# Centre rows alternate in a set: spread in two matmuls a quarter, samples written row by row

## The chip, the cores and the metric

The kernel runs on one core of one Trainium2 chip. The metric is device time in microseconds (us) of one execution. TensorE (PE in the rows; PEld is its weight load), VectorE (DVE), ScalarE (ACT), GpSimd (POOL) and SyncE (SP, which issues the DMAs) run side by side and wait for each other by semaphores.

## The reference

The input is 8 images of 32 channels, 128x128, float32. Two blocks follow each other, each with a residual:

```
x = x + L0(gn(x))      # 16 Fourier modes along rows and along columns, and a 1x1 mix
x = x + L1(gn(x))      # modulated deformable 3x3 convolution
```

`gn` with 32 groups of 32 channels is a normalization of each channel of each image. The second block takes nearly all of the time and is what the change touches:

```
om   = conv3x3(x, w_om) + b_om          # 27 channels: 9 dy, 9 dx, 9 masks
ys   = dy + ky + row - 1 ;  xs = dx + kx + col - 1
vals = bilinear(x, ys, xs) * sigmoid(mask)          # for every pixel and tap
out  = einsum('bckhw,ock->bohw', vals, weight) + bias
```

## The kernel before, in words

Images are taken four at a time (`IPG`), two groups (`g_count`), so that 4 x 32 channels fill 128 partitions. After a first stage (statistics, Fourier terms, mix), the second block walks over *sets*. A set is a pair of sample rows (`TILE_R` = 2); there are 65 sets a group (`NSET`), 130 in all. For every set the bilinear sampling is done as matrix products:

- `offsets` (L1025) makes the 27 channels of offsets and masks on TensorE; ScalarE adds the bias into `om_s`; `turn_offsets` (L1029 to L1037) multiplies `om_s` by the 0/1 matrix `perm_s`, which turns pixels into partitions and puts channels in the order wanted. It takes one matmul for each of the two rows. VectorE (L803) subtracts a grid from the result, ScalarE makes hat functions of it (L628, L610), and GpSimd multiplies the hats of y and x (`product`, L485) into `prod`, which VectorE transposes (L761) into `PT`.
- `spread` (L971 to L984) lays the 25 coefficients of a sample out over the positions of a window of 6 x 10 pixels: a product with the 0/1 matrix `sel_s`, which depends on whether the sample's centre row is the first or the second of the tile. It runs three times a set (`ROUNDS`, one for each kx). A set has `ROWS` = 6 *places*, each a pair of output row and ky; `MGROUPS` lists the runs of places that share a centre row: 2, 3 and 1 places. For each run there is a matmul for each half `h` of the columns and each quarter `u` of the partitions, that is 3 x 8. A place has 64 columns (4 images x 16 tiles), so that the runs have 128, 192 and 64. The result goes to `pE` and is copied to `A` by ScalarE (h = 0) and VectorE (h = 1).
- `turn_rows` (L1010 to L1018) transposes windows of the image, four at a time, into `pR`; ScalarE copies them to `XT`.
- `gather` (L987 to L1005) multiplies windows by coefficients: for each tile of 4 pixels, image and half one matmul with 32 output partitions and 72 columns (kx, pixel, place), written next to each other in `pV`. It comes in three parts (`VGROUPS`: 5, 5 and 6 tiles; 80, 80 and 96 recorded matmuls). `evacuate` (L306) tells how ScalarE (L591) and VectorE (L791) copy `pV` to `VS`: they read with a step of 6 elements and write runs of 60 or 72 elements.
- `convolve` (L1039 to L1052) multiplies `VS` by the weights, 36 matmuls of 128 columns; the moving operand is read in runs of 4 elements, 12 apart. VectorE adds bias and residual (L784), and the result is stored.

The kernel is float32 throughout. The trace records each product with data two times, as two weight loads and two matmuls; a transpose is recorded once. The order of TensorE's work in one step is written out by hand in `step` (L1054): spread 0 of set N, convolution of set N-3, gather part 0 of set N-1, turn_rows 0, spread 1, turn_rows 1, offsets of N+3, gather part 1, turn_rows 2, spread 2, turn_offsets of N+3, turn_rows 3, gather part 2. The convolution waits, among others, until VectorE's L803 of the step before has read the bank that it shares (`sub_done`).

The steps are held in two loops, one a group, of 28 iterations with two steps each (`steps`, L270; `UNROLL` = 2); the other 18 sets are written out in straight code before, between and behind the loops.

Of the kernel before, what the change touches and what calls it, by code (L numbers as in the profile page):

```python
# [15 lines left out]
C = 32  # L16
H = W = 128
IPG = 4
P = IPG * C
HW = H * W  # L20
MODES = 16
KS = 3
TAPS = KS * KS
# [3 lines left out]
TILE_R, TILE_C = 2, 4  # L27
WIN_R, WIN_C = TILE_R + 2 * REACH, TILE_C + KS - 1 + 2 * REACH
REG = WIN_R * WIN_C
HALF = P // 2  # L30
# [3 lines left out]
NT = W // TILE_C  # L34
NTP = NT // 2
# [3 lines left out]
OMC = 3 * TAPS  # L39
OMG = IPG * C  # L40
SQ = NSH * NSH
BLK = 32
QUADS = P // BLK
ROWS = KS * TILE_R
PB = ROWS * IPG
# [4 lines left out]
TAPC = KS * TILE_C * ROWS  # L50
# [2 lines left out]
NG = len(VGROUPS)  # L53
PRE = ROWS // 2

MGROUPS = [(0, 2, 0), (2, 5, 1), (5, 6, 0)]

KYS = ((1, 0, 2), (0, 1, 2))
RING = 4
TCH = 4  # L60
TPC = NTP // TCH
# [9 lines left out]
def build(nc, g_count, x, wxr, wxi, wyr, wyi, mixt, mixb, womt, bom, wct, biasc,  # L71
          dft, inv, ident_d, perm, sel, cols, gtab, out):
    ctx = ExitStack()
    with ctx:
        def sb(name, shape, dt=fp32):
            return ctx.enter_context(nc.sbuf_tensor(name, shape, dt))
# [21 lines left out]
        A, VS, XT = areas[0:2], areas[2:4], areas[4:6]  # L98
# [13 lines left out]
        bom_s = sb("bom_s", [OMG, 1])  # L112
        wc = sb("wc", [P, TAPS, 2 * C])
        bias_s = sb("bias_s", [P, 1])
        perm_s = sb("perm_s", [P, TILE_R, OMC * IPG])
        sel_s = sb("sel_s", [P, TILE_R * KS, HALF])
        cols_s = sb("cols_s", [P, 4 + NSH])
        stats = sb("stats", [P, NXC, 6])
# [15 lines left out]
        om_s = sb("om_s", [P, PX])  # L134
# [8 lines left out]
        at = [0]  # L143
# [37 lines left out]
        pV = [pb(f"pV{i}", [P, 512]) for i in range(2)]  # L181
        pMR = pb("pMR", [P, 2 * 512])
        pM, pR = pMR[:, 0:512], pMR[:, 512:1024]
        pO = pMR[:, :].rearrange("p (r n) -> p r n", r=2)[:, :, PX:PX + W]
# [121 lines left out]
        def evacuate(q, gi, h):  # L306

            t0, t1 = VGROUPS[gi]
            x = KS * TILE_C
            dst = VS[q].rearrange("p (m x) -> p m x", m=ROWS)[:, :, (h * NTP + t0) * x:(h * NTP + t1) * x]  # L310
            return dst, pV[h][:, 0:(t1 - t0) * TAPC].rearrange("p (x m) -> p m x", m=ROWS)

        def expanded(q, r, h):

# [17 lines left out]
        def _(sp):  # L332
# [8 lines left out]
            for dst, src in ((dft_s[:, :], dft), (inv_s[:, :], inv),  # L341
                             (wsp[:, 0, :], wxr.rearrange("c o f -> c (o f)")),
                             (wsp[:, 1, :], wxi.rearrange("c o f -> c (o f)")),
                             (wsp[:, 2, :], wyr.rearrange("c o f -> c (o f)")),
                             (wsp[:, 3, :], wyi.rearrange("c o f -> c (o f)")),
                             (cols_s[:, :], cols),
                             (perm_s[:, :, :], perm), (sel_s[:, :, :], sel)):
                sp.dma_start(dst, src).then_inc(const_ld, 16)
            for g in range(1, g_count):
                load_images(g)  # L350
# [2 lines left out]
            for b in range(IPG):  # L353
                r, m = slice(b * C, (b + 1) * C), slice(b * C, b * C + OMC)
# [4 lines left out]
                o = b % 2 * C  # L359
                sp.dma_start(wc[r, :, o:o + C], wct.rearrange("k c o -> c k o")).then_inc(blocks_ld, 16)  # L360
            for ky in range(KS):
                r, k = slice(ky * C, (ky + 1) * C), slice(ky * KS, (ky + 1) * KS)
# [75 lines left out]
            with sp.If(far > 0):  # L438
# [17 lines left out]
                for i in range(images):  # L456
                    m = g_sem[i // IPG]
# [438 lines left out]
        def _(pe):  # L896
            mm = nc.tensor.matmul
# [74 lines left out]
            def spread(n, rn, buf):  # L972

                pe.wait_ge(pt_done, n * ROUNDS + (rn + 1))
                wait(pe, e_act, n * ROUNDS + rn)
                wait(pe, e_dve, n * ROUNDS + rn)
                for first, end, i2 in MGROUPS:
                    for h, u in itertools.product(range(2), range(QUADS)):
                        part = slice(u * BLK, (u + 1) * BLK)
                        src = PT[part, buf, :].rearrange("p (m b t) -> p m b t", m=ROWS, b=IPG)  # L980
                        o = pE[h * HALF:(h + 1) * HALF, u * 512:u * 512 + EPX] \
                            .rearrange("p (m b t) -> p m b t", m=ROWS, b=IPG)
                        last = mm(o[:, first:end], sel_s[part, i2 * KS + rn, :],  # L983
                                  src[:, first:end, :, h * NTP:(h + 1) * NTP], start=True, stop=True)  # L984
                last.then_inc(e_done, 1)

            def gather(n, q, gi):  # L987

                if gi == 0:
                    pe.wait_ge(e_act, n * ROUNDS + ROUNDS)  # L990
                    pe.wait_ge(e_dve, n * ROUNDS + ROUNDS)
                    pe.wait_ge(xt_done, n * TCH + TCH)
                wait(pe, v_act, n * NG + gi)
                wait(pe, v_dve, n * NG + gi)
                pe.nop(nofuse=True)
                t0, t1 = VGROUPS[gi]
                for t in range(t0, t1):
                    o = (t - t0) * TAPC
                    for b, h in itertools.product(range(IPG), range(2)):
                        part = slice(h * HALF, h * HALF + REG)  # L1000
                        at = (b * NTP + t) * TAPC
                        last = mm(pV[h][b * C:(b + 1) * C, o:o + TAPC],  # L1002
                                  XT[q][part, t * P + b * C:t * P + (b + 1) * C],
                                  A[q][part, at:at + TAPC], start=True, stop=True)
                last.then_inc(v_done, 1)  # L1005
# [23 lines left out]
            def turn_offsets(n):  # L1029

                pe.wait_ge(om_act, n + 1)
                for i in range(TILE_R):
                    o = pM[:, 0:OMC * IPG * TILE_R].rearrange("p (f k i b) -> p i f k b", f=3 * KS, k=KS, i=TILE_R)
                    last = mm(o[:, i], om_s[:, i * W:(i + 1) * W],  # L1034
                              perm_s[:, i, :].rearrange("p (f k b) -> p f k b", f=3 * KS, k=KS),
                              start=True, stop=True)
                last.then_inc(omT_done, 1)  # L1037

            def convolve(c, q):  # L1039

                pe.nop(nofuse=True)
                for k, (ky, kx) in enumerate(itertools.product(range(KS), range(KS))):
                    for i, r in itertools.product(range(TILE_R), range(2)):

                        at = TILE_R * KYS[i].index(ky) + i
                        own = at < PRE
                        m = at + PRE if own else at - PRE
                        src = VS[q if own else 1 - q].rearrange("p (m t k j) -> p m t k j", m=ROWS, t=NT, k=KS)
                        part = slice(r * HALF, (r + 1) * HALF)
                        last = mm(pO[i * HALF:(i + 1) * HALF, r, :].rearrange("p (t j) -> p t j", t=NT),  # L1050
                                  wc[part, k, :], src[part, m, :, kx, :], start=(k == 0), stop=(k == TAPS - 1))
                last.then_inc(conv_done, 1)  # L1052

            def step(N, s, on, place):  # L1054
# [68 lines left out]
def constants():  # L1123
# [14 lines left out]
    cols[:, 3] = BN_EPS  # L1138
    cols[:, 4:] = np.arange(NSH) - REACH
    a["cols"] = cols  # L1140
    perm = np.zeros((IPG, BLK, TILE_R, 3, KS, KS, IPG), np.float32)
    for f, kx, i, k, b in itertools.product(range(3), range(KS), range(TILE_R), range(KS), range(IPG)):
        perm[b, f * TAPS + KYS[i][k] * KS + kx, i, f, kx, k, b] = 1
    a["perm"] = perm.reshape(P, TILE_R, OMC * IPG)
    sel = np.zeros((QUADS, BLK, TILE_R, KS, HALF), np.float32)
    for u, sy, sx, i, kx in itertools.product(range(QUADS), range(NSH), range(NSH), range(TILE_R), range(KS)):
        sel[u, sy * NSH + sx, i, kx, (i + sy) * WIN_C + u + kx + sx] = 1
# [36 lines left out]
```

## Time and profile before

| | us |
|---|---|
| median of 2 runs | 2763.61 (2759.2 to 2768.01) |
| profiled execution, device time | 2763.84 |
| its span | 2762.0 |
| PE busy | 2020.7 (73%) |
| PEld busy | 1550.6 (56%) |
| DVE busy | 1338.0 (48%) |
| ACT busy | 1089.8 (39%) |
| POOL busy | 851.8 (31%) |

TensorE is the busiest engine, with 67513 matmuls and as many weight loads of the 153257 instructions of the whole program. Its granted clock was 0.876 of full speed on average. Busy time of matmuls is a union: up to eight that use different parts of the array are in flight together, so the mean time of one (300 ns) says little of how fast they follow each other; the timeline, which merges instructions of a line that follow each other and gives their count, tells that. "Issue" in a chain or behind a row is time in which the engine waited for nothing that the profile shows.

### The profile page before, as it was taken

The page shows a single profiled execution, that of the slowest core. Times are in us where ns is not written, and L with a number is a line of the kernel's source. Part 1 is how long each engine was busy: PE and PEld are TensorE (multiplying, and loading weights), DVE is VectorE, ACT ScalarE, POOL GpSimd, SP SyncE. Part 2 cuts the span into 40 slices and gives each one's busy share as a digit, 9 for nine tenths or more (in the row PEclk, how much of TensorE's full clock was granted, in tenths as well). Part 3 has the DMA queues.
Part 4 walks back from the last instruction along what each step waited for, and adds up shares of the span by engine and source line. Part 5 has one row for each costly group of instructions (what it writes and reads, how often), then busy time and mean ns, then how long its engine had stood idle before and what let it go on. Part 6 is the DMA issues. An engine that isn't in the chain of part 4 may idle for free.

```text
span 2762.0 us, 153257 instructions
## 1 busy us (share of the span) xinstructions
PE 2020.7 (73%) x67513; PEld 1550.6 (56%) x67513; DVE 1338.0 (48%) x2068; ACT 1089.8 (39%) x1858; POOL 851.8 (31%) x893
## 2 busy tenths in 40 slices
PE   8562777767677777777877887777777778777776
PEld 3310555556556655655656665666666556566665
DVE  8694444434444444444444554444444444444453
ACT  0023444334334334334433544444444444444443
POOL 0000433223323333333333443333333333333331
PEclk9697799888888888888888999999989999999998
DMA  7046322212212122122222222222222222222220
GB/s 268 31 192 278 88 66 61 58 52 65 54 52 67 52 54 66 52 53 66 54 64 55 78 69 68 66 56 66 68 54 67 67 68 68 54 67 68 60 64 26
DMA packets 162286, 205.88 MB, mean 75 GB/s; under 512 B 20288, under 2 KB 136672, under 8 KB 157536
## 3 DMA queue, kind: packets, MB, share of 16 engines
q1 hardware_dynamic: 161632, 195.34, 23.9%
q8 instruction: 633, 10.37, 1.7%
q14 instruction: 21, 0.17, 0.0%
HBM read 143.05 MB, written 52.22 MB: 71 GB/s over the span
## 4 chain that ended last, share of the span: by engine, by line
PE 63%; issue 22%; DVE 7%; ACT 3%; DVEq 2%; DMA 1%; ACTq 0%; SPq 0%
PE pV L1002 16%; PE pMR L1050 14%; PE pE L983 12%; PE pMR L1013 9%; PE pMR L1025 7%; PE pMR L1034 3%; DVE big L738 2%; DVE big L761 2%; ACT big L597 2%; DVE big L803 1%; ACT big L610 1%; DMA xh_scratch<-win 1%; DVEq L738 1%; DVE stats L673 1%; PE pV L938 1%
## 5 line engine op out<-in xcount | busy, mean ns | idle before, releaser
L485 POOL TENSOR_TENSOR prod<-big 128x600 f32<-128x600 f32 (+1 forms) x489 | 503.2, 1038 | 1330.2 <-DVE big L761 1316.9
L983 PE MATMUL pE<-big,sel_s 32*64 32x128 f32 (+2 forms) x18720 | 462.2, 302 | 352.0 <-issue 349.7
L983 PEld LDWEIGHTS pE<-big,sel_s 32*64 32x64 f32 x18720 | 365.5, 143 | 453.7 <-issue 427.7
L1002 PE MATMUL pV<-big 60*32 60x72 f32 x33280 | 477.1, 232 | 146.5 <-issue 144.7
L775 DVE COPY big<-pE 128x768 f32<-128x768 f32 x390 | 368.9, 946 | 378.8 <-PE pE L983 370.8
L791 DVE COPY big<-pV 128x360 f32<-128x360 f32 (+1 forms) x390 | 217.4, 557 | 675.1 <-PE pV L1002 675.1
L1002 PEld LDWEIGHTS pV<-big 60*32 60x32 f32 x33280 | 382.8, 106 | 272.0 <-issue 271.0
L604 ACT ACTIVATE big<-pE 128x768 f32<-128x768 f32 x390 | 331.9, 851 | 504.8 <-PE pE L983 503.8
L591 ACT ACTIVATE big<-pV 128x360 f32<-128x360 f32 (+1 forms) x390 | 191.6, 491 | 779.0 <-PE pV L1002 778.9
L1050 PE MATMUL pMR<-big,wc 64*64 64x128 f32 x9216 | 404.2, 339 | 45.9 <-DVE big L803 28.1
L1050 PEld LDWEIGHTS pMR<-big,wc 64*64 64x64 f32 x9216 | 363.8, 176 | 66.6 <-issue 57.4
L1013 PE MATMUL pMR<-ident,big 128*128 128x128 f32 x2080 | 341.6, 285 | 51.2 <-issue 26.6
L761 DVE STREAM_TRANSPOSE big<-prod 128x768 f32<-128x768 f32 x390 | 377.8, 969 | 0.0
L597 ACT ACTIVATE big<-pMR 128x512 f32<-128x512 f32 x520 | 308.0, 592 | 16.3 <-PE pMR L1013 12.8
L1013 PEld LDWEIGHTS pMR<-ident,big 128*128 128x128 f32 x2080 | 223.1, 142 | 100.7 <-ACT big L597 35.4
L515 POOL COPY big<-win 128x960 f32<-128x960 f32 x260 | 248.7, 986 | 0.3 <-DMA win<-xh_scratch 0.3
L1025 PE MATMUL pMR<-big,wom 96*32 96x256 f32 x3120 | 200.3, 389 | 56.1 <-DMA big<-xh_scratch 44.9
L784 DVE SCALAR_TENSOR_TENSOR outs<-pMR,bias_s,x1r 128x256 f32<-128x256 f32 x128 | 62.0, 484 | 273.2 <-PE pMR L1050 273.2
L525 POOL TENSOR_TENSOR big<-big,msk 128x360 f32<-128x360 f32 x130 | 107.0, 823 | 270.4 <-ACT big L628 270.4
L1025 PEld LDWEIGHTS pMR<-big,wom 96*32 96x32 f32 x3120 | 88.2, 110 | 128.8 <-issue 81.2
L803 DVE TENSOR_TENSOR big<-pMR,cols_s 128x720 f32<-128x720 f32 x130 | 116.6, 897 | 50.9 <-ACT msk L637 50.9
L628 ACT ACTIVATE big<-big,cols_s 128x720 f32<-128x720 f32 x130 | 115.3, 887 | 0.0
(70 smaller groups left out, 901.7 us busy)
## 6 DMA issues: line engine op xcount, KB each, us to landing
big<-xh_scratch SPq DMA_DIRECT2D x390, 136.0 KB
win<-xh_scratch SPq DMA_DIRECT2D x130, 408.0 KB, 4.0
xh_scratch<-win SPq DMA_DIRECT2D x32, 544.0 KB, 2.7
big<-in_x SPq DMA_DIRECT2D x16, 1024.0 KB, 15.5
x_scratch<-big SPq DMA_DIRECT2D x16, 1024.0 KB, 3.9
x1r<-x_scratch SPq DMA_DIRECT2D x256, 64.0 KB, 3.3
out<-outs SPq DMA_DIRECT2D x256, 64.0 KB, 2.1
xh_scratch<-zero SPq DMA_DIRECT2D x4, 204.0 KB, 2.7
```

Of the source, the lines that this page charges most:

```text
L485: return nc.gpsimd.tensor_tensor(prod[:, buf, at:at + m, 0:SQ].rearrange("p m (a b) -> p m a b", a=NSH), hy.to_broadcast(shape), hx.to_bro ...
L515: last = nc.gpsimd.tensor_copy(strips[:, 1 - s % 2, :, h, 0:REG].rearrange("p t (r x) -> p t r x", r=WIN_R), tiles_of(1 - s % 2, h))
L597: nc.scalar.activation(XT[q][:, k * 512:(k + 1) * 512], pR[:, :], ACT.Copy).then_inc(xt_done, 1)
L604: nc.scalar.activation(*expanded(q, r, 0), ACT.Copy).then_inc(e_act, 1)
L761: nc.vector.transpose(PT[:, buf, :], prod[:, buf, :, :].rearrange("p m k -> p (m k)")) \
L775: nc.vector.tensor_copy(*expanded(q, r, 1)).then_inc(e_dve, 1)
L791: nc.vector.tensor_copy(*evacuate(1 - q, r, 1)).then_inc(v_dve, 1)
L983: last = mm(o[:, first:end], sel_s[part, i2 * KS + rn, :], src[:, first:end, :, h * NTP:(h + 1) * NTP], start=True, stop=True)
L1002: last = mm(pV[h][b * C:(b + 1) * C, o:o + TAPC], XT[q][part, t * P + b * C:t * P + (b + 1) * C], A[q][part, at:at + TAPC], start=True, st ...
L1013: last = nc.tensor.transpose(pR[:, u * P:(u + 1) * P], strips[:, q, k * TPC + u, :, :].rearrange("p h x -> p (h x)"), ident[:, :])
L1025: last = mm(pM[b * C:(b + 1) * C, 0:PX], wom[:, kx, :], wino[0:KS * C, q, b, :, x0:x0 + W], start=(kx == 0), stop=(kx == KS - 1))
L1050: last = mm(pO[i * HALF:(i + 1) * HALF, r, :].rearrange("p (t j) -> p t j", t=NT), wc[part, k, :], src[part, m, :, kx, :], start=(k == 0), ...
```

## The change

`MGROUPS` and `KYS` go, and `PLACES` lists the six places (output row, ky) so that their centre rows alternate; in `spread` the places 0, 2, 4 share one and 1, 3, 5 the other. So there are two matmuls instead of three for each quarter and half, each of three places, 192 columns. The moving operand and the output step over every other place, in runs of 64 columns in the output.

`turn_offsets` now fills its output in three matmuls (`FILLS`: the row that is turned, and the places that it fills) instead of two, with 108, 72 and 36 columns in place of 108 and 108. `perm_s` has one matrix for both rows.

`gather` writes the samples by place and kx, then column: consecutive output elements of a matmul (the six places) now lie a whole place apart, 60 elements in the parts with 5 tiles and 72 in that with 6. With it `evacuate` reads `pV` in order and writes `VS` in 18 runs of 20 or 24 elements, and `convolve` reads whole rows of 128.

```diff
-MGROUPS = [(0, 2, 0), (2, 5, 1), (5, 6, 0)]
-KYS = ((1, 0, 2), (0, 1, 2))
+PLACES = ((1, 0), (0, 0), (0, 1), (0, 2), (1, 2), (1, 1))
+FILLS = ((0, 1, 4), (1, 4, 6), (1, 0, 1))
...
         def evacuate(q, gi, h):
-            x = KS * TILE_C
-            dst = VS[q].rearrange("p (m x) -> p m x", m=ROWS)[:, :, (h * NTP + t0) * x:(h * NTP + t1) * x]
-            return dst, pV[h][:, 0:(t1 - t0) * TAPC].rearrange("p (x m) -> p m x", m=ROWS)
+            dst = VS[q].rearrange("p (n x) -> p n x", x=W)[:, :, (h * NTP + t0) * TILE_C:(h * NTP + t1) * TILE_C]
+            return dst, pV[h][:, 0:(t1 - t0) * TAPC].rearrange("p (n x) -> p n x", n=ROWS * KS)
...
-                for first, end, i2 in MGROUPS:
+                for i2 in range(TILE_R):
                     for h, u in itertools.product(range(2), range(QUADS)):
-                        last = mm(o[:, first:end], sel_s[part, i2 * KS + rn, :],
-                                  src[:, first:end, :, h * NTP:(h + 1) * NTP], start=True, stop=True)
+                        last = mm(o[:, i2::TILE_R], sel_s[part, i2 * KS + rn, :],
+                                  src[:, i2::TILE_R, :, h * NTP:(h + 1) * NTP], start=True, stop=True)
...
                 for t in range(t0, t1):
-                    o = (t - t0) * TAPC
+                    x = slice((t - t0) * TILE_C, (t - t0 + 1) * TILE_C)
                     for b, h in itertools.product(range(IPG), range(2)):
-                        last = mm(pV[h][b * C:(b + 1) * C, o:o + TAPC],
+                        o = pV[h][b * C:(b + 1) * C, 0:(t1 - t0) * TAPC]                             .rearrange("p (m k x) -> p k x m", m=ROWS, k=KS)
+                        last = mm(o[:, :, x, :],
                                   XT[q][part, t * P + b * C:t * P + (b + 1) * C],
                                   A[q][part, at:at + TAPC], start=True, stop=True)
...
             def turn_offsets(n):
-                for i in range(TILE_R):
-                    o = pM[:, 0:OMC * IPG * TILE_R].rearrange("p (f k i b) -> p i f k b", f=3 * KS, k=KS, i=TILE_R)
-                    last = mm(o[:, i], om_s[:, i * W:(i + 1) * W],
-                              perm_s[:, i, :].rearrange("p (f k b) -> p f k b", f=3 * KS, k=KS),
+                o = pM[:, 0:3 * KS * PB].rearrange("p (f m b) -> p f m b", f=3 * KS, m=ROWS)
+                place_of = perm_s[:, :].rearrange("p (f m b) -> p f m b", f=3 * KS, m=ROWS)
+                for i, m0, m1 in FILLS:
+                    last = mm(o[:, :, m0:m1], om_s[:, i * W:(i + 1) * W], place_of[:, :, m0:m1],
                               start=True, stop=True)
...
-                        at = TILE_R * KYS[i].index(ky) + i
+                        at = PLACES.index((i, ky))
-                        src = VS[q if own else 1 - q].rearrange("p (m t k j) -> p m t k j", m=ROWS, t=NT, k=KS)
+                        src = VS[q if own else 1 - q].rearrange("p (m k x) -> p m k x", m=ROWS, k=KS)
-                        last = mm(pO[i * HALF:(i + 1) * HALF, r, :].rearrange("p (t j) -> p t j", t=NT),
-                                  wc[part, k, :], src[part, m, :, kx, :], start=(k == 0), stop=(k == TAPS - 1))
+                        last = mm(pO[i * HALF:(i + 1) * HALF, r, :], wc[part, k, :], src[part, m, kx, :], start=(k == 0), stop=(k == TAPS - 1))
```

The order of the work in a step, the waits, the loops and the copies' sizes stay as they were.

## Rows read from the trace of the kernel before

**Rows 1.** The page: span, instruction queue, and the chain that ended last.
```profile
span 2762.0 us, 153257 instructions
...
q8 instruction: 633, 10.37, 1.7%
...
PE 63%; issue 22%; DVE 7%; ACT 3%; DVEq 2%; DMA 1%; ACTq 0%; SPq 0%
```

**Rows 2.** Windows: loop 1, loop 2, straight code (start:end, us, busy (x count), clock).
```profile
701.10:1110.60 409.50, 303.13 (x10327) 241.60 (x10324) 176.53 (x240) 162.83 (x280) 130.07 (x135) 0.84 0.22 58
1875.90:2280.40 404.50, 304.98 (x11359) 245.22 (x11352) 190.52 (x264) 175.45 (x308) 143.32 (x150) 0.91 0.24 64
1529.00:1591.40 62.40, 52.23 (x2068) 41.20 (x2069) 34.39 (x49) 31.77 (x57) 26.03 (x27) 1.00 0.27 73
```

**Rows 3.** Timeline of PE, straight code: start, length, what, count [idle before].
```profile
1526.84 0.44 PE L1002 MATMUL pV<-big 60*32 60x72 f32 x19 [1.07 <-issue]
1527.20 0.91 PE L983 MATMUL pE<-big,sel_s 32*64 32x128 f32 x48
1528.95 2.20 PE L1050 MATMUL pMR<-big,wc 64*64 64x128 f32 x72 [0.83 <-issue]
1531.08 1.08 PE L1002 MATMUL pV<-big 60*32 60x72 f32 x80
1532.08 0.66 PE L1013 MATMUL pMR<-ident,big 128*128 128x128 f32 x4
1532.67 0.79 PE L983 MATMUL pE<-big,sel_s 32*64 32x128 f32 x28
1534.46 0.66 PE L983 MATMUL pE<-big,sel_s 32*64 32x192 f32 x20 [1.00 <-issue]
```

**Rows 4.** Timeline of PE in loop 1, around the loop's jump.
```profile
1102.19 0.33 PE L1002 MATMUL pV<-big 60*32 60x72 f32 x8 [2.19 <-issue]
1106.50 1.34 PE L983 MATMUL pE<-big,sel_s 32*64 32x128 f32 x25 [3.98 <-issue]
1109.50 1.12 PE L983 MATMUL pE<-big,sel_s 32*64 32x192 f32 x23 [1.66 <-issue]
...
1126.05 0.89 PE L983 MATMUL pE<-big,sel_s 32*64 32x128 f32 x42 [1.63 <-issue]
```

**Rows 5.** Timeline of PE in loop 2, an iteration's second set and the jump.
```profile
2260.70 2.32 PE L1050 MATMUL pMR<-big,wc 64*64 64x128 f32 x72 [0.97 <-DVE big L803]
...
2265.44 0.49 PE L1013 MATMUL pMR<-ident,big 128*128 128x128 f32 x3 [1.15 <-issue]
...
2271.16 0.69 PE L1034 MATMUL pMR<-perm_s,om_s 128*128 128x108 f32 x4
2271.69 0.60 PE L1013 MATMUL pMR<-ident,big 128*128 128x128 f32 x4
...
2273.37 0.89 PE L1002 MATMUL pV<-big 60*32 60x72 f32 x65 [0.68 <-issue]
2278.91 1.59 PE L983 MATMUL pE<-big,sel_s 32*64 32x128 f32 x48 [4.65 <-issue]
```

**Rows 6.** Groups of instructions by form: count, busy us, mean ns, idle before.
```profile
L1002 PE MATMUL pV<-big 60*32 60x72 f32 x33280 | 477.1, 232 | 146.5 <-issue 144.7 <-DVE big L791 1.4
...
L983 PE MATMUL pE<-big,sel_s 32*64 32x192 f32 x6240 | 278.3, 357 | 51.9 <-issue 51.0
...
L983 PE MATMUL pE<-big,sel_s 32*64 32x128 f32 x6240 | 218.1, 315 | 287.4 <-issue 286.1 <-DVE big L775 0.8
...
L983 PE MATMUL pE<-big,sel_s 32*64 32x64 f32 x6240 | 178.1, 234 | 12.7 <-issue 12.6
...
L791 DVE COPY big<-pV 128x360 f32<-128x360 f32 x260 | 138.4, 532 | 388.8 <-PE pV L1002 388.8
...
L803 DVE TENSOR_TENSOR big<-pMR,cols_s 128x720 f32<-128x720 f32 x130 | 116.6, 897 | 50.9 <-ACT msk L637 50.9
...
L791 DVE COPY big<-pV 128x432 f32<-128x432 f32 x130 | 79.0, 607 | 286.3 <-PE pV L1002 286.3
```

More of the change, by code:

```diff
@@ L114, in build @@
         bias_s = sb("bias_s", [P, 1])
-        perm_s = sb("perm_s", [P, TILE_R, OMC * IPG])
+        perm_s = sb("perm_s", [P, 3 * KS * PB])
         sel_s = sb("sel_s", [P, TILE_R * KS, HALF])
@@ L346, in _ @@
                              (cols_s[:, :], cols),
-                             (perm_s[:, :, :], perm), (sel_s[:, :, :], sel)):
+                             (perm_s[:, :], perm), (sel_s[:, :, :], sel)):
                 sp.dma_start(dst, src).then_inc(const_ld, 16)
@@ L1140, in constants @@
     a["cols"] = cols
[L1141 to L1144, printed above, removed]
+    perm = np.zeros((IPG, BLK, 3, KS, ROWS, IPG), np.float32)
+    for f, kx, m, b in itertools.product(range(3), range(KS), range(ROWS), range(IPG)):
+        perm[b, f * TAPS + PLACES[m][1] * KS + kx, f, kx, m, b] = 1
+    a["perm"] = perm.reshape(P, 3 * KS * PB)
     sel = np.zeros((QUADS, BLK, TILE_R, KS, HALF), np.float32)
```

## The prediction

> **What bounds the kernel now.** I read the page first: its chain of work that ended last is 63% PE and 22% "issue" [rows 1]. So TensorE carries the end, and a fifth of the span it stands still without waiting for a semaphore that the profile shows. Where these stops lie, the timeline of PE tells. Some stand at a change of work; the longest of the others come in the middle of a run of equal matmuls that depend on nothing new: 1.07 us inside gather part 2, then 1.00 us inside spread 1 [rows 3]. Between these two stand 19+48+72+80+4+28 = 251 matmuls with as many weight loads, 502 recorded instructions, and by the code some ten waits and register instructions. The instruction queue moved 10.37 MB in 633 packets [rows 1], 16.4 KB each, and 10.37 MB over 153257 instructions is 68 bytes for each. So a packet carries about 250 instructions (my estimate: 64 bytes, 256 instructions, as the profile does not record all), and the stops are two packets apart. I read them as TensorE running dry: its code is streamed anew each time round, and a dense stretch of small matmuls eats a packet faster than the next one comes. The windows give the pace: straight code takes 62.4 us for 4 sets at full clock, 15.6 us a set, 15.1 ns for each of the 4137 matmuls and loads. Loop 2 takes 404.5 us for 22 sets, 36.8 us an iteration of two, at clock 0.91; loop 1 409.5 us for 20 sets, 41.0 us an iteration, at clock 0.84 [rows 2]. Both loops run the same work. What differs is the stops: at the jump back PE waits 3.98 us in loop 1 and 4.65 us in loop 2, but loop 1 stops besides for 2.19 us eight matmuls ahead of the jump, for 1.66 us 25 matmuls behind it, and for 1.63 us in the next spread 0 [rows 4]; loop 2 shows 1.15 and 0.68 us in its second set [rows 5]. With 2.19 and 3.98 us of rest nearly on end, TensorE falls to the lower of its two clock levels (a mean of 0.84 is two thirds of the time at 2.4 GHz and one third at 1.2).
>
> **What the change takes away, in instructions.** Spread has 24 matmuls a round and gets 16, each recorded as two loads and two matmuls: 3 rounds x 8 x 4 = 96 fewer. turn_offsets gets one matmul more, +4. That is 92 of about 1034 recorded instructions a set [rows 2], or 8.9%; an iteration goes from about 2118 (waits included) to 1934.
>
> **Spread on TensorE itself.** A round lasts from 1527.20 to 1528.11, 0.91 us [rows 3]. Its columns stay the same: 16 x (128+192+64) = 6144 = 32 x 192 (16 recorded matmuls for each of the three old groups, 32 new). If instructions set its length, it loses 16 x 19 ns = 0.3 us; if columns do, nothing. Gather passes 80 matmuls from 1531.08 to 1532.08, 12.5 ns each [rows 3], with as many loads, so 48 could pass in 0.6 us; and 128 more columns raise the mean of one from 234 to 357 ns [rows 6]. It is columns, and I take 0. A gain in spread 0 would in part be lost anyway: convolution behind it waits for VectorE's L803, 0.97 us [rows 5], and that comes from the end of gather part 2 by a copy of 607 ns and 897 ns of L803 [rows 6], whatever spread does.
>
> **turn_offsets.** Four matmuls of 108 columns take 2271.16 to 2271.69, 0.53 us [rows 5], 133 ns each; the transposes with 128 columns take (1532.67 - 1532.08)/4 = 148 ns [rows 3]. Two more cost from 0 (hidden in a wait for code) to 2 x 133 ns = 0.27 us a set, 35 us in all. Nearest is 0.15 us, and it lies in a stretch that runs dry before or behind it, so I charge 0.1 us a set in straight code and put it into the loops' sums below.
>
> **Evacuation and convolution.** The copy of 360 elements takes 532 ns, that of 432 takes 607 [rows 6]: 1.04 ns an element, with PSUM read at a step of 6. L803, which reads each PSUM value in place, takes 897 ns for 720: (897-607)/288 = 1.01 ns. A read in order saves 0 to 0.03 x 360 = 11 ns; I take 0. Convolution's 72 matmuls took 2.20 us [rows 3], 31 ns each; the whole-row read saves from 0 to the gap to what its columns need. At the rate of spread, 0.91 us / 6144 = 0.148 ns a column with eight tiles in flight, four tiles need 0.296 x 128 = 38 ns. It is faster already, so 0.
>
> **Gather's strided write.** The trace before has no matmul whose neighbouring outputs lie apart one by one. Lower bound: nothing. The nearest row is turn_offsets, which writes runs of four elements with gaps, and at 133 ns for 108 columns it is not slower than the transposes that write in order. Upper bound: a write that halves or quarters the rate of columns. At 0.148 ns a column the 72 columns need 10.7 ns of the 12.5 that a matmul now takes. Twice that is 21.3 ns, +8.8 x 256 = +2.3 us a set; four times is 42.6 ns, +7.7 us a set. I take no cost, since neither the read with a step (L791) nor the write with gaps (turn_offsets) shows one. The Trainium skill ("PSUM — Partial Sum Buffer", section Specifications (TRN2)) speaks against that: it gives PSUM lines of 8 bytes and says that any non-contiguous pattern slows matmuls significantly. The rows of turn_offsets show no such cost for runs of 16 bytes; of single elements no row here tells. By the rows the sum is the 2595 below, by the page the first rival's 2725 to 3430.
>
> **Where the stops go.** The saving is in waiting for code, and in the straight code it is 92 x 15.1 ns = 1.4 us a set less the 0.1 above: 1.3 us, within the roughly 2 us of stops in a set [rows 3]. 18 sets give -23 us.
>
> In the loops the place of the packets' boundaries decides. Loop 1 runs dry 25 matmuls into an iteration, about 53 instructions with the waits, and then 53 + 8 x 256 = 2101, which is the stop eight matmuls ahead of the end at 2118 [rows 4]: the reading holds. Before loop 1 lie 5 sets with spread and 8 turn_offsets, so its start moves forward in the code by 5 x 96 - 8 x 4 = 448 = 256 + 192 instructions, and its first boundary comes 192 later in it: at 245, and the last to 1781, 153 ahead of the jump. Both costly stops (2.19 + 1.66 us) fall away, the jump's stays. Of the others (1.63 us) about half goes. The clock gains as well: a third of an iteration is now at half rate, and with 3.9 us less rest about 2.5 us of it should go, worth 1.2 us of work. Sum: -3.85 - 0.8 - 1.2 + 0.2 (turn_offsets) = -5.7 us an iteration, x 28 = -160 us.
>
> Loop 2 runs dry after one transpose of its second set's turn_rows 0 [rows 5], instruction 1475, so its first boundary is at about 190. Its start moves forward by 448 + 184 + 9 x 92 = 1460 = 5 x 256 + 180 instructions, so its first boundary goes to 190 + 180 - 256 = 114, and the last one to 1906, 28 ahead of the jump at 1934: where loop 1 has its 2.19 us now. So loop 2 gains some 2.0 us of other stops (1.15, 0.68 and their like in its first set) and pays 2.2 us and some clock for the new place: +0.5 us, x 28 = +14 us.
>
> Together -23 - 160 + 14 = -169 us. Against the profiled execution's span of 2762.0 that is 2593; 1.8 us lie around it (2763.84, and the median of the runs is 2763.61), so 2595.
>
> The Trainium skill ("Runtime: NRT & Kernel Launch", section Instruction fetch mechanics) says that code comes in blocks of 256 instructions, that crossing one is mostly hidden and that a taken branch breaks the prefetch. The trace agrees on the blocks and on the jump (3.98 and 4.65 us), not on "hidden".
>
> **Rivals.** *First, the write is slow.* It needs the single strided elements to cost where groups of four do not. At twice the columns' time, +2.3 us a set less about 1.3 us of stops that it fills, +130 us: 2725. It decides for "slower" (over 2819) when a set pays 1.7 us beyond what the stops cover: 3.0 us / 256 = 11.7 ns more, 24 ns a matmul, 2.3 times the columns' 10.7. At four times, +6.4 x 130: 3430. If the array's columns are cheaper than spread suggests, twice is almost covered by the stops: 2625.
>
> *Second, the stops are not code.* If "issue" were a cost that each place has in itself, 92 fewer instructions would only move it to L803 (0.97 us) and to ScalarE's copies; then about 0.3 us a set is left: 2725. Against it: the same work has other stops in each loop, two packets apart.
>
> *Third, boundaries fall elsewhere than counted.* The shift rests on counted instructions. Worst, both loops get loop 1's present places, with two packets' worth less to wait for: -2.0 and +2.2 us an iteration, 2745. Best, both get good ones: loop 2 gains 3 us, 2500.
>
> **Numbers.** Forecast as worked out (2520 to 2660) 0.48; its better end 0.07; the write at up to twice 0.16, half of it still over 2% faster; the write at 2.3 times or more 0.14; stops not code or boundaries badly placed 0.15, a third of it over 2% faster. Faster by over 2% (2708): 0.48 + 0.07 + 0.08 + 0.05 = 0.68; slower 0.14; within 2% 0.18. A measurement of this kernel tells less than 2% from no change with difficulty. The range, 2500 to 2800, leaves out the slow write and the best tail.
>
> **What would show it.** L983 with 12480 matmuls, all of 192 columns, and a round still near 0.9 us; L1034 with 6 a set; L1002 still 12.5 ns a matmul in the timeline (near 21 if the write is slow, with a mean well over 232 ns); fewer packets on the instruction queue, about 633 - 130 x 92 / 256 = 586; loop 1 near 35 us an iteration with no stop just ahead of the jump, loop 2 near 37 with one. I am wrong if L1002's runs grow, or if the stops keep their sum.

## The result, and the profile after

| | us |
|---|---|
| before, median | 2763.61 |
| changed, median of 2 runs | 2620.68 (2619.18 to 2622.18) |
| ratio | 0.948, 95% interval 0.941 to 0.955 |
| span of the profiled execution | 2617.3 |

The change makes the kernel 5.2% faster; 2595 was forecast. The page of the changed kernel has 11960 instructions fewer, 62 packets less on the instruction queue (its columns: packets, MB, share), and a chain with 19% of "issue" where before had 22% [rows 1]:

```profile
span 2617.3 us, 141297 instructions
...
q8 instruction: 571, 9.36, 1.5%
...
PE 65%; issue 19%; DVE 8%; ACT 4%; DVEq 2%; DMA 1%; ACTq 0%; SPq 0%
```

The same three kinds of stretch as in [rows 2], each laid along whole iterations: 20 sets of loop 1, 22 of loop 2, 4 of the straight code (columns: start:end, us, busy and count of PE, PEld, DVE, ACT and POOL, granted clock, DMA share, GB/s).

```profile
582.00:946.90 364.90, 287.62 (x9404) 221.43 (x9404) 174.40 (x240) 160.76 (x281) 130.12 (x135) 0.88 0.25 64
1805.90:2210.00 404.10, 311.15 (x10346) 231.73 (x10345) 190.49 (x265) 176.64 (x309) 143.31 (x150) 0.92 0.24 64
1360.20:1421.00 60.80, 52.29 (x1891) 39.20 (x1887) 34.60 (x49) 32.20 (x57) 26.79 (x28) 1.00 0.28 77
```

An iteration of loop 1 takes 36.5 us in place of 41.0; one of loop 2 36.7 as before (36.8); a set of the straight code 15.2 in place of 15.6. Over all 26 iterations between the first and the last jump back, loop 1 takes 36.25 us in place of 41.05 and loop 2 36.8 in both. So of the 145 us of span 126 (28 x 4.5, by the windows) to 134 (28 x 4.8, by all iterations) come out of loop 1 alone and nothing out of loop 2. What is left, 12 to 19 us, is put down to the 18 sets written out, 0.6 to 1.0 us each; the four of the window show 0.4.

TensorE's own work has hardly changed, as the groups by form show against [rows 6]: a gather matmul, which now writes elements 60 or 72 apart, takes 232 ns as it did, and the copy that now reads in order takes 532 ns as it did.

```profile
L1002 PE MATMUL pV<-big 60*32 60x72 f32 x33280 | 470.7, 232 | 89.4 <-issue 87.1 <-DVE big L790 1.6
L982 PE MATMUL pE<-big,sel_s 32*64 32x192 f32 x12480 | 429.6, 365 | 319.3 <-issue 318.4 <-DVE big L774 0.8
...
L790 DVE COPY big<-pV 128x360 f32<-128x360 f32 x260 | 138.4, 532 | 383.9 <-PE pV L1002 383.9
```

Timeline of PE around the jump of loop 1 (start, length, line, count, idle before):

```profile
924.04 0.87 PE L982 MATMUL pE<-big,sel_s 32*64 32x192 f32 x20
926.44 0.57 PE L982 MATMUL pE<-big,sel_s 32*64 32x192 f32 x12 [1.53 <-issue]
...
937.16 0.91 PE L982 MATMUL pE<-big,sel_s 32*64 32x192 f32 x32
937.99 0.86 PE L1035 MATMUL pMR<-perm_s,om_s 128*128 128x108 f32 x6
938.68 0.63 PE L1013 MATMUL pMR<-ident,big 128*128 128x128 f32 x4
939.25 1.31 PE L1002 MATMUL pV<-big 60*32 60x72 f32 x96
945.12 1.59 PE L982 MATMUL pE<-big,sel_s 32*64 32x192 f32 x32 [4.56 <-issue]
```

Against [rows 4] the stop of 2.19 us eight matmuls ahead of the jump and that of 1.66 us behind it are gone: gather's 96 and spread's 32 run through. The stop at the jump is longer, 4.56 in place of 3.98 us, and the one in the next spread 0 is still there (1.53, was 1.63). And of loop 2:

```profile
2018.71 1.11 PE L1002 MATMUL pV<-big 60*32 60x72 f32 x85
2022.38 0.34 PE L1002 MATMUL pV<-big 60*32 60x72 f32 x11 [2.56 <-issue]
2026.62 1.59 PE L982 MATMUL pE<-big,sel_s 32*64 32x192 f32 x32 [3.90 <-issue]
...
2042.52 0.69 PE L1002 MATMUL pV<-big 60*32 60x72 f32 x41 [0.52 <-issue]
```

Here is the new stop, 11 matmuls ahead of the jump: 11 x 2 recorded instructions and the waits behind them, where the count of the prediction had put it (28 instructions). It stands there, 11 matmuls ahead, at all 27 jumps of this loop, and lasts from 0.3 to 2.8 us, 1.84 us in the mean. With it the stop at the jump is shorter, 3.90 in place of 4.65 us [rows 5]. The last row is the same part of gather in the next iteration's first set: the count has a boundary there too, 114 + 3 x 256 = 882 instructions behind the jump.

### The profile page after: what moved, and what is told of

Read it like the earlier page. It is cut to its first block, busy times and chain, and to the rows that moved or that the text cites. A ratio compares the mean times of both kernels' runs of the same rounds, so it can differ in the third digit from the quotient of the medians.

```text
span 2617.3 us, 141297 instructions
## 1 busy us (share of the span) xinstructions
PE 1998.2 (76%) x61533; PEld 1456.0 (56%) x61533; DVE 1332.1 (51%) x2068; ACT 1088.3 (42%) x1858; POOL 851.8 (33%) x893
## 4 chain that ended last, share of the span: by engine, by line
PE 65%; issue 19%; DVE 8%; ACT 4%; DVEq 2%; DMA 1%; ACTq 0%; SPq 0%
PE pV L1002 17%; PE pMR L1050 15%; PE pE L982 11%; PE pMR L1013 9%; PE pMR L1025 7%; PE pMR L1035 4%; DVE big L737 2%; ACT big L596 2%; DVE big L760 2%; DVE big L802 1%; ACT big L609 1%; DMA xh_scratch<-win 1%; DVEq L737 1%; DVE stats L672 1%; PE pV L937 1%
## 5 line engine op out<-in xcount | busy, mean ns | idle before, releaser
L982 PE MATMUL pE<-big,sel_s 32*64 32x192 f32 x12480 | 429.6, 365 | 319.3 <-issue 318.4
L1002 PE MATMUL pV<-big 60*32 60x72 f32 x33280 | 470.7, 232 | 89.4 <-issue 87.1
L982 PEld LDWEIGHTS pE<-big,sel_s 32*64 32x64 f32 x12480 | 252.5, 142 | 405.6 <-issue 391.0
L1050 PEld LDWEIGHTS pMR<-big,wc 64*64 64x64 f32 x9216 | 356.2, 174 | 107.5 <-issue 107.1
L1013 PEld LDWEIGHTS pMR<-ident,big 128*128 128x128 f32 x2080 | 229.8, 146 | 105.8 <-ACT big L596 63.4
L1035 PEld LDWEIGHTS pMR<-perm_s,om_s 128*128 128x128 f32 x780 | 98.9, 194 | 40.1 <-issue 35.5
## 6 DMA issues: line engine op xcount, KB each, us to landing
big<-in_x SPq DMA_DIRECT2D x16, 1024.0 KB, 15.5
```

The costliest lines, as they stand in the source:

```text
L982: last = mm(o[:, i2::TILE_R], sel_s[part, i2 * KS + rn, :], src[:, i2::TILE_R, :, h * NTP:(h + 1) * NTP], start=True, stop=True)
L1002: last = mm(o[:, :, x, :], XT[q][part, t * P + b * C:t * P + (b + 1) * C], A[q][part, at:at + TAPC], start=True, stop=True)
L1013: last = nc.tensor.transpose(pR[:, u * P:(u + 1) * P], strips[:, q, k * TPC + u, :, :].rearrange("p h x -> p (h x)"), ident[:, :])
L1050: last = mm(pO[i * HALF:(i + 1) * HALF, r, :], wc[part, k, :], src[part, m, kx, :], start=(k == 0), stop=(k == TAPS - 1))
```

## The experiments

Each stands beside runs of the kernel before on its own chip; the chips differ (before took 2766.4, 2739.3 and 2797.6 us on the three), so ratios are compared, or kernels of the same call.

**The layouts apart from the spread.** First the changed kernel with the old gather, copies and convolution:

```diff
-            return dst, pV[h][:, 0:(t1 - t0) * TAPC].rearrange("p (n x) -> p n x", n=ROWS * KS)
...
+            return dst, pV[h][:, 0:(t1 - t0) * TAPC].rearrange("p (x m) -> p m x", m=ROWS)
...
-                        last = mm(o[:, :, x, :],
+                        last = mm(pV[h][b * C:(b + 1) * C, o:o + TAPC],
...
```

> The changed kernel with gather, evacuation and convolution as they were before: the samples are written next to each other, the copies read PSUM with a step of 6, the convolution reads runs of 4. The instruction count and every packet boundary are those of the changed kernel. If fewer instructions make the gain: 2620 us as changed, within 15. If the rows layout brings part of it (a faster copy or convolution), this one is slower than 2620 by that part; if the strided write costs something that the gain hid, it is faster than 2620.

Measured: 2597.51 us, ratio 0.939 (0.937 to 0.942), 8 us below the range of 2620 within 15. Then the other half, the kernel before with the new layouts alone:

> The kernel before with only the rows layout (strided gather write, copies in order, convolution of whole rows); spread keeps its three groups and turn_offsets its two matmuls. Instruction count as before. If fewer instructions make the gain: as before, 2763 us within 15. If the layout makes it: near 2620. If the strided write costs and was hidden: above 2780.

Measured: 2767.0 us beside 2766.44, ratio 1.0006 (0.9991 to 1.0022), over ten runs. So all of the gain is with the spread (and the third matmul of turn_offsets that belongs to it), and the layouts bring nothing. Its gather, written with a stride, and its copy, against [rows 6]:

```profile
L1002 PE MATMUL pV<-big 60*32 60x72 f32 x33280 | 472.0, 231 | 144.9 <-issue 143.4 <-DVE big L790 1.3
...
L790 DVE COPY big<-pV 128x360 f32<-128x360 f32 x260 | 138.4, 532 | 373.6 <-PE pV L1002 373.6
```

231 ns for a matmul and 532 for a copy: nothing in either. The first run left a question, as it was faster than the changed kernel had been. So that was run again:

> The changed kernel itself, timed beside the others. 2620 us if the 23 us by which the kernel with alternating spread alone was faster (2597.5) belong to the rows layout; 2600 to 2610 if they are a matter of the day and the few runs.

Measured: 2582.41 us, below both values, but on a chip on which before took 2739.29, so that only the ratio speaks: 0.942 (0.939 to 0.945). The intervals of 0.939 and 0.942 overlap; by these two runs a cost of the strided write of up to some 0.7% can't be told from none. The run before them, on one chip, leaves 0.2%, and both layouts were timed beside each other again below, without loops.

**The code moved, nothing changed.** The kernel before with 60 transposes more while TensorE waits for the images anyway:

```diff
             pe.wait_ge(ident_ld, 16)
+            for _ in range(120 // 2):
+                nc.tensor.transpose(pM[:, 0:P], ident[:, :], ident[:, :])
```

> The kernel before, with 60 transposes of the identity (120 instructions, about 8 us of TensorE's time while it waits for the images) ahead of everything, which moves the code of both loops by 119 instructions against the packets and changes nothing in them. Loop 1's first boundary goes from 53 to 190, its last from 19 to 136 ahead of the jump, which is where loop 2 has them now; loop 2's goes from 190 to 71. If the place of the boundaries sets the stops: loop 1 41.0 -> about 37 us an iteration, loop 2 36.8 -> about 38.5, together about 2690 us (2660 to 2730). If only the number of instructions counts, or the columns: as before, 2763 within 10.

Measured: 2737.15 us, ratio 0.990 (0.987 to 0.993): faster by 1.0%, but above the range of 2660 to 2730. Windows over 20 sets of each loop:

```profile
582.78:960.93 378.15, 280.68 (x10325) 223.73 (x10320) 173.20 (x240) 158.53 (x280) 130.02 (x135) 0.89 0.24 62
1787.62:2179.57 391.95, 302.11 (x10324) 244.35 (x10320) 176.30 (x240) 162.36 (x280) 129.99 (x135) 0.85 0.23 60
```

The loops have changed places: loop 1 takes 37.8 us an iteration (was 41.0), loop 2 39.2 (was 36.8), with not one instruction in them changed. 120 instructions at the start of the program are worth 3.2 us an iteration one way and 2.4 us the other. That the stops come where packets end is shown by this. The sum was expected at 2690, since loop 1 was put at about 37 and loop 2 at its new boundary (71) at 38.5. The timeline of loop 2 shows why it came out at 39.2:

```profile
1792.04 1.54 PE L985 MATMUL pE<-big,sel_s 32*64 32x128 f32 x37 [4.36 <-issue]
1795.07 0.50 PE L985 MATMUL pE<-big,sel_s 32*64 32x64 f32 x11 [1.49 <-issue]
```

After 4.36 us at the jump TensorE gets through 37 matmuls and stands again for 1.49 us: a first boundary soon behind the jump costs a second stop. It does so behind each of the 27 jumps of this loop (1.1 to 1.8 us) and of loop 1 before (1.4 to 1.9 us): the packets' own times in the traces show that the next packet begins only 0.3 to 1.0 us after TensorE goes on.

These times show the cause directly. Every packet of the instruction queue has 16384 bytes. In the kernel before, between 500 and 2200 us, all 165 stops of over 0.3 us in the middle of a run of equal matmuls end 2.2 to 3.0 us after the last packet began; a packet takes about 1.1 us (median), and TensorE goes on 1.2 to 1.7 us after it has landed. In the two kernels without loops that follow below, the packets begin at least 3.3 us apart between 500 and 2200 us, 3.9 and 4.0 us in the median, so that one is under way at a time.

**The third matmul put back.** The changed kernel, all layouts and the order of places kept, but three places cut into 2 and 1:

```diff
-                for i2 in range(TILE_R):
+                for i2, first, end in ((0, 0, 4), (1, 1, 6), (0, 4, 5)):
...
-                        last = mm(o[:, i2::TILE_R], ...
+                        last = mm(o[:, first:end:TILE_R], ...
```

> The changed kernel with spread's first group of three places cut in two (2 and 1 places), so that there are again 24 matmuls of 128, 192 and 64 columns: the instruction count of before plus 4 a set, columns, layouts and the order of the places as changed. If instructions make the gain: 2780 us (2750 to 2810), loop 1 near 41 us an iteration with a stop at its start, loop 2 near 37.3. If the alternating places or the row layout make it: 2620.

Measured: 2810.32 us, ratio 1.017 (1.013 to 1.021), at the upper end of the range. All of the gain is gone and 44 us more, which are loop 2's. Loop 1 is back at 40.6 us an iteration, loop 2 at 38.9 with its first boundary at 114 (37.3 was expected):

```profile
611.39:1017.71 406.32, 302.37 (x10370) 245.55 (x10360) 174.33 (x240) 161.81 (x280) 130.04 (x135) 0.84 0.22 58
1874.80:2263.82 389.02, 296.42 (x10362) 242.50 (x10360) 174.30 (x240) 160.95 (x280) 130.03 (x135) 0.86 0.23 61
```

The columns are those of the changed kernel, so the gain is one of instructions and not of how the places lie. But the boundaries in the loops have moved with the count, and this run doesn't tell the two apart; the kernels without loops do.

**Loop 2 moved in the changed kernel.** Matmuls of one spread are issued again in a straight set between the loops (they write the same values once more):

```diff
-                    spread(N, 0, q)
+                    spread(N, 0, q, 44 if isinstance(N, int) and N == NSET else 0)
```

> The changed kernel with 44 matmuls of 64 columns of one spread issued again in straight code between the loops (176 instructions, about 1 us once), which moves loop 2's code and nothing else: its first packet boundary goes from 114 to 194, its last from 28 ahead of the jump to 204. If the place of the boundaries sets the stops, the stop of about 1.8 us in gather part 2 ahead of the jump goes and loop 2 falls from 36.8 to about 34.5 us an iteration: 2560 us (2545 to 2590). If the place doesn't matter: 2621.

Measured: 2615.49 us, ratio 0.955 (0.954 to 0.957), where the changed kernel had 0.942 on the same chip: 33 us or 1.3% slower, not faster. This was a miss. The windows (loop 1, which didn't move, and loop 2, ten iterations each) give 36.1 and 36.9 us an iteration:

```profile
575.47:936.04 360.57, 283.21 (x9400) 216.60 (x9400) 174.31 (x241) 160.49 (x281) 130.07 (x135) 0.90 0.24 65
1719.70:2088.63 368.93, 287.70 (x9400) 221.54 (x9400) 173.34 (x241) 161.00 (x281) 130.10 (x135) 0.88 0.24 63
```

On that chip the changed kernel took 35.9 and 35.8:

```profile
465.23:824.64 359.41, 284.70 (x9400) 218.43 (x9400) 174.15 (x241) 160.39 (x281) 130.08 (x135) 0.89 0.24 65
1601.76:1959.70 357.94, 281.77 (x9400) 210.56 (x9400) 173.17 (x241) 160.26 (x281) 130.06 (x135) 0.92 0.24 66
```

So the 33 us are loop 2's. Its timeline (gather is L1010 in this kernel) shows what it has in place of the stop ahead of the jump:

```profile
1742.09 0.25 PE L1010 MATMUL pV<-big 60*32 60x72 f32 x1 [2.49 <-issue]
...
1761.98 1.58 PE L982 MATMUL pE<-big,sel_s 32*64 32x192 f32 x32 [4.91 <-issue]
```

The stop ahead of the jump has gone, but that at the jump is 4.91 us and not 3.90, and inside the iteration a boundary now falls one matmul ahead of gather's end, behind the densest run of instructions, and costs 2.49 us (1.93 in the mean). A boundary close ahead of the jump is thus no loss by itself: it makes the jump's own stop shorter. All 27 jumps of each loop show it, with the packets that begin while TensorE stands there:

| loop | last boundary ahead of the jump, instructions by the count | stop at the jump, median (range), us | packets that begin |
|---|---|---|---|
| before, loop 1 | 19 | 3.60 (3.4 to 4.0) | 1 |
| changed, loop 2 | 28 | 3.72 (3.4 to 4.0) | 1 |
| third matmul put back, loop 1 | 57 | 3.64 (3.3 to 3.9) | 1 |
| before, loop 2 | 136 | 4.77 (4.6 to 5.1) | 2 |
| before and moved, loop 1 | 136 | 4.94 (4.6 to 5.5) | 2 |
| changed, loop 1 | 153 | 4.95 (4.4 to 5.8) | 2 |
| changed and moved, loop 2 | 204 | 4.67 (4.1 to 5.3) | 2 |
| third matmul put back, loop 2 | 220 | 4.51 (4.0 to 5.1) | 2 |
| before and moved, loop 2 | 255 | 4.32 (3.6 to 5.0) | 2 (at two jumps 1) |

A packet that begins alone takes about 1.1 us; the second of two, which begins 0.5 to 1.1 us behind the first (medians of the loops), takes 1.6 to 2.0, and TensorE goes on about 1.7 us after it has landed in either case. So the stop is longer because the packet that ends it begins behind another or is slower beside it. That the first of them is the code behind the loop's end, fetched for nothing, is my reading; the traces don't say which code a packet holds.

**Fewer jumps.** Four sets to an iteration on TensorE:

```diff
-            steps(pe, step, UNROLL)
+            steps(pe, step, RING)
```

> The changed kernel with four sets to an iteration in TensorE's loops in place of two; the other engines' loops as they are. 28 jumps fewer. An iteration of two sets takes 36.2 and 36.8 us in the loops and 30.4 in straight code, so a jump costs about 6.1 us with the slow clock behind it. If jump and fetch bind: 2620 - 28 x 6.1 = 2450 us (2410 to 2500). If the stop at the jump is a wait for another engine's work, which would come late elsewhere too: above 2550.

Measured: 2454.26 us, ratio 0.897 (0.894 to 0.900). That it lies next to the 2450 expected is luck: this chip is faster than the one that the sum started from. Beside the changed kernel's 2582.41 us here, 28 jumps fewer give 128 us and not 170, that is 4.6 us a jump and not 6.1. And none at all:

```diff
-            steps(pe, step, UNROLL)
+            for N in range(-3, SETS + 2):
+                live = [0 <= N + k < SETS for k in (0, -1, -3, 3, 2, 1, -2)]
+                live[2] = live[2] and (N - 3) % NSET < NPAIR
+                live[6] = live[6] and (N - 2) % NSET < NPAIR
+                step(N, N % RING, live, lambda n: divmod(n, NSET))
```

> The changed kernel with TensorE's 133 steps all written out, no loop; the other engines' loops as they are. If the jumps and the clock that falls behind them are what the loops add: 112 sets at 15.2 us in place of 18.3, 2620 - 347 = 2275 us (2240 to 2350), clock near 1.0 throughout. If code that is never run twice is fetched more slowly, or another engine is next: above 2400.

Measured: 2281.28 us, ratio 0.833 (0.831 to 0.835). It beats both kernels, with the same work on every engine. Again the chip helps it to its number: beside 2582.41 it is 301 us, not 347, or 5.6 us for each of the 54 jumps taken. Its page shows the clock at nine tenths or more from the seventh slice to the last but one, and 84 packets fewer than the changed kernel's 571, though all its code is different code: jumping back saves no fetch.

```profile
PEclk9599589999999999999999999999999999999998
...
q8 instruction: 487, 7.98, 1.4%
...
PE 70%; issue 16%; DVE 5%; ACT 4%; DVEq 2%; DMA 1%; ACTq 0%; SPq 0%
```

**The change without loops.** Three kernels on one chip, all written out: the one before, the changed one, and the changed one with the old layouts.

> The kernel before with TensorE's 133 steps all written out, no loop. Against it the changed kernel in the same form (2281 us) shows what the change is worth where no jump and no fixed place of a packet boundary plays in. If TensorE waits for its code: between 2281 + 125 x 0.45 = 2337 (the 15.6 us a set of before's straight stretch against 15.15 of the changed kernel written out) and 2281 + 125 x 1.3 = 2440. If only the jumps and the places of the boundaries cost, and 92 instructions less are worth nothing by themselves: 2260 to 2285.

> The changed kernel written out again, on the same chip as the two others: 0.833 of the kernel before, 2281 us.

> The changed kernel with gather, copies and convolution as before (samples next to each other), all steps written out. In the loops this layout was 0.3% faster than the changed one, by different chips. If the strided write costs or the rows layout gains anything, it shows here beside the changed kernel written out: same within 0.3% if the layout is worth nothing; 10 to 25 us faster if the strided write costs.

Measured: 2469.76, 2315.45 and 2316.48 us; as ratios 0.886 (0.881 to 0.891), 0.829 (0.824 to 0.834) and 0.832 (0.827 to 0.838). Without loops the change is worth 2469.76 - 2315.45 = 154 us, 6.2%, or 1.2 us for each of the 130 sets. The first time lies above its 2337 to 2440, which started from 2281 on another chip; the difference lies within the 56 to 159 us that these mean. The layouts are worth 1 us in 2316; the four runs of each kernel spread over 18 and 19 us, so that a few us can't be excluded. The 10 to 25 us for a strided write that costs didn't show. The queue's packets of the first, and windows of 1000 us of the first two:

```profile
q8 instruction: 533, 8.73, 1.5%
...
800.00:1800.00 1000.00, 825.65 (x30999) 661.10 (x30990) 520.43 (x721) 479.28 (x842) 390.73 (x406) 0.94 0.26 70
...
800.00:1800.00 1000.00, 859.85 (x30334) 647.06 (x30326) 558.35 (x776) 519.83 (x905) 420.64 (x436) 0.98 0.28 74
```

In the same time before issues 30999 matmuls and the changed kernel 30334, 2% apart, though the latter does 8% more sets with them (776 of VectorE's instructions against 721). TensorE gets its instructions at nearly one rate, 16.1 and 16.5 ns for each matmul or load; what counts is how many of them a set needs. The packets agree: 533 against 487 is 46 fewer, and 130 x 92 / 256 = 46.7 were counted. With 12 of VectorE's instructions a set, as in the windows above, a set takes 16.6 and 15.5 us. Of the 1.2 us between them 0.7 us are less standing still and 0.4 us less busy time of TensorE. The latter comes with the higher clock (0.98 against 0.94), and what holds the clock down in the first comes from its stops too:

```profile
1214.71 0.43 PE L983 MATMUL pE<-big,sel_s 32*64 32x128 f32 x3
1217.26 1.41 PE L983 MATMUL pE<-big,sel_s 32*64 32x128 f32 x45 [2.13 <-issue]
```

Three matmuls into a spread it stands for 2.13 us, and the 45 behind them last 1.41 us, at a granted clock of 0.60, where 48 take 0.91 at full clock [rows 3].

## Why the prediction was right, point by point

*The sum.* 2595 was forecast and 2621 measured. The mechanism was right, but the small distance owes something to luck: loop 1 gave 26 to 34 us less than forecast and the straight code 4 to 11 us less, loop 2 was 13 to 15 us better.

*What bounds the kernel.* Right. That TensorE waits for its own code was read from stops two packets apart; moving the code alone made loop 1 faster by 3.2 us and loop 2 slower by 2.4 us an iteration, the stops end when a packet has landed, and putting the third matmul back took the gain away.

*Spread's columns.* Right: nothing was charged, and a round of 32 matmuls takes the 0.91 us of the 48 [rows 3]. The mean of one is 365 ns, close to the 357 of the form with 192 columns [rows 6].

*turn_offsets.* Right, 0.15 us taken: its six take 938.68 - 937.99 = 0.69 us in place of 0.53 [rows 5].

*Evacuation, convolution, the strided write.* Right at 0, by two comparisons (1.0006 in the loops, 1 us in 2316 without). The write was the least certain term and the first rival, with 0.14 for "slower". It stayed at 232 ns with elements 60 and 72 apart. The page "PSUM — Partial Sum Buffer" of the Trainium skill (section Specifications (TRN2)), which speaks of a significant slowdown, isn't borne out for this float32 matmul; for other types no run here tells.

*The second rival*, that stops only move elsewhere, fell: written out, 1.2 us a set was kept. The wait for L803 ahead of the convolution, which could have eaten it, is still there (0.97 us in loop 2) but hasn't grown, since spread 0 in front of it takes as long as before. Written out, a little did move there: ahead of the convolution TensorE stands for 91.7 us in the kernel before and for 115.8 us in the changed one, 0.2 us a set.

*The straight code*: -23 us forecast (1.3 us a set), and 12 to 19 us are left for it (the window shows 0.4 us a set), so the term was somewhat too large there; without loops the change is worth 1.2 us a set, which is the forecast's.

*Loop 1*: -160 us forecast, -126 to -134 measured. The mechanism was right, both stops that were to fall fell, 3.8 us as forecast. Three terms of the -5.7 us an iteration were mis-sized. The stop at the jump was taken as unchanged; in the mean of all iterations it goes from 3.67 to 4.99 us, 1.3 us more (the 3.98 us of rows 4 is the longest of its 27). Of the stop in spread 0 half, 0.8 us, was to go, and 0.1 went (1.85 to 1.74 in the mean). Against that the other stops gave 0.8 us that was not counted, and the work itself ran 1.4 us faster where 1.0 was forecast: 4.0 us less of an iteration passes at the lower of TensorE's two clock levels (12.4 to 8.4), and 2.5 was taken.

*Loop 2*: +14 us forecast, -1 measured. The place of the new stop was right to a few instructions, but its price was taken without the jump's: in the mean 1.8 us come (2.2 forecast), 1.1 us of the jump's stop go (none forecast), and 1.4 us of the other stops (2.0 forecast). That is 0.6 us less of standing still, yet an iteration takes 36.8 us as before; turn_offsets takes 0.3 us of it, and where the rest goes stays open.

*The third rival*, boundaries placed otherwise than counted, fell too: each came where the count had put it. But which place is good was less clear than the prediction had it. It ranked a boundary just ahead of the jump as costly; moving it away made the kernel 1.3% slower, since the stop at the jump grew by 1.0 us (3.65 to 4.66 in the mean on that chip) and the stop in gather came back elsewhere. Costly are a boundary soon behind the jump (loop 1 before, 41.0 us) and one in or behind gather.

*The packets*: 586 were forecast and 571 came. The count holds without loops (46 fewer); in the loops 62 fell away, since a loop fetches more than its instructions and how much depends on its place.

## What to carry to other kernels

Where an engine runs many small instructions and stands still in the middle of a run of equal ones, with no semaphore behind it, count the instructions between the stops and compare with the instruction queue's packets: if they fit, each instruction has a price whatever its columns, and merging matmuls pays even where TensorE's columns stay the same. A loop then costs more than it saves: here TensorE stood for 3.3 to 5.8 us at a jump back, each jump saved was worth 4.6 us (four sets to an iteration) to 5.6 us (none at all), and writing the steps out was worth another 301 us beside the change's 157 on the same chip (2739.29, 2582.41, 2281.28). And where loops stay, a small edit anywhere ahead of them shifts all the packet boundaries in them, which is worth 2.4 to 3.2 us an iteration here: a gain of one or two per cent may be the shift and not the edit.

## What the runs showed of the hardware that was not expected

- A loop's code is fetched again in every iteration, and with it more than without a loop: 571 packets with loops, 487 written out, for the same work.
- Without loops the instruction queue's packets of 16384 bytes begin at least 3.3 us apart, about 4 us in the median, and after a stop in a run of equal matmuls TensorE goes on 1.2 to 1.7 us after one has landed. A run of instructions that is gone through faster than that, as gather's (two every 12.5 ns), ends in a stop whatever its columns.
- The stop at a jump depends on where the last boundary lies: 3.6 to 3.7 us (medians) with 19 to 57 instructions between it and the jump, 4.3 to 5.0 with 136 to 255, where a second packet begins in the stop.
- TensorE writes single float32 elements 240 or 288 bytes apart as fast as it writes them in a row: 231 or 232 ns for 72 columns, taking the eight parts of the array in turn, one every 12.5 ns or so.
- Matmuls of 72 and of 36 columns on the whole array cost nearly the same: from start to start (medians) the two of 72 in turn_offsets take 194 ns and the two of 36 take 190 ns, with 263 and 265 ns as their means.

```profile
L1035 PE MATMUL pMR<-perm_s,om_s 128*128 128x108 f32 x260 | 62.6, 322 | 1.9 <-ACT om_s L618 1.9
...
L1035 PE MATMUL pMR<-perm_s,om_s 128*128 128x72 f32 x260 | 47.0, 263 | 0.0
L1035 PE MATMUL pMR<-perm_s,om_s 128*128 128x36 f32 x260 | 47.0, 265 | 0.0
```
